# Deformable convolution block: nine 3x3 taps in 32x32 tiles, another order up to the offsets, and window sums in slabs with four product rows on GpSimd

## The reference

```python
h = gelu(conv1x1(x, proj1)); u = h
h = dwconv5x5(h, conv0)                      # pad 2
# deformable convolution, 8 groups of 8 channels, 3x3 points
xproj = h @ inproj + b                       # the "values"
x1 = gelu(layernorm(dwconv3x3(h)))
offset = x1 @ off_w + off_b                  # 2 x 9 x 8 per pixel
m = softmax(x1 @ mask_w + mask_b)            # over the 9 points
out = sum over points of m * bilinear(xproj, point + offset)
attn = conv1x1(out @ outproj)
x = conv1x1(u * attn, proj2) + shortcut
t = t + gru_like_attention(layernorm(t))     # 256 tokens per image
t = t + moe_top2_of_8(layernorm(t))          # 64 wide experts
```

## Time and profile before

| | us |
|---|---|
| median of 3 runs | 105.86 (105.59 to 106.24) |
| the profiled execution | 105.47 |
| its span, first to last instruction | 103.8 |
| mean granted TensorE clock | 0.984 of 2.4 GHz |
| PE / DVE / ACT / POOL busy | 95.0 / 70.0 / 44.5 / 27.6 |

### The profile page before, as it was taken

The page is one execution under the profiler, slowest core; times in us unless marked ns, Lnnn a source line. Parts: engine busy times, 40 slices in busy tenths (PEclk is TensorE's granted clock), DMA queues, the critical chain, the costliest instruction groups (busy, mean ns, idle before and its releaser), DMA issues.

```text
span 103.8 us, 2125 instructions
## 1 busy us (share of the span) xinstructions
PE 95.0 (91%) x843; PEld 64.3 (62%) x847; DVE 70.0 (67%) x157; ACT 44.5 (43%) x96; POOL 27.6 (27%) x37
## 2 busy tenths in 40 slices
PE   4999969999989999998999999899899999889990
PEld 1545526477646698995777776448596886664340
DVE  1359676824128999999999733477942569946871
ACT  1362054379449670000000204588842798796000
POOL 7295900000001919057897400000000000500000
PEclk9999999999859999999999999999999999999999
DMA  1999000000146526530000000000000000000002
GB/s 41 392 350 352 8 0 6 0 6 0 51 133 209 192 70 189 163 115 0 0 3 0 0 0 9 0 0 0 0 0 0 0 6 0 0 0 0 0 3 101
DMA packets 3226, 6.22 MB, mean 60 GB/s; under 512 B 528, under 2 KB 1296, under 8 KB 3216
## 3 DMA queue, kind: packets, MB, share of 16 engines
q1 hardware_dynamic: 2784, 4.67, 13.8%
q10 hardware_dynamic: 432, 1.42, 3.8%
HBM read 5.16 MB, written 0.93 MB: 59 GB/s over the span
## 4 chain that ended last, share of the span: by engine, by line
PE 61%; DVE 21%; issue 8%; ACT 6%; POOL 1%; DVEq 0%
PE ps L1121 60%; DVE prod L902 3%; DVE ym L873 2%; DVE terms L882 2%; ACT prod L712 2%; POOL prod L542 1%; ACT prod L768 1%; DVE lmax L857 1%; DVE smax L949 1%; DVE psum_p L887 1%; DVE prod L983 1%; DVE prod L987 1%; DVE prod L823 1%; PE ps L1449 1%; DVE rsum L893 1%
## 5 line engine op out<-in xcount | busy, mean ns | idle before, releaser
L1121 PE MATMUL ps<-prod,wts 128*128 128x256 f32 (+1 forms) x116 | 25.4, 394 | 1.2 <-POOL prod L542 0.6
L1121 PEld LDWEIGHTS ps<-prod,wts 128*128 128x128 f32 (+1 forms) x116 | 16.6, 174 | 8.2 <-POOL prod L542 2.6
L1121 PE MATMUL ps<-terms,wts 64*128 64x256 f32 (+4 forms) x104 | 17.4, 354 | 0.9 <-ACT prod L768 0.5
L1121 PEld LDWEIGHTS ps<-terms,wts 128*128 128x128 f32 (+1 forms) x104 | 13.8, 189 | 3.5 <-ACT prod L768 0.9
L902 DVE TENSOR_TENSOR prod<-v_win,ps 128x1280 f32<-128x1280 f32 x10 | 14.3, 1462 | 0.0
L542 POOL TENSOR_TENSOR prod<-prod 128x512 f32<-128x512 f32 x9 | 11.5, 1278 | 5.3 <-DVE prod L902 4.8
L533 POOL TENSOR_TENSOR terms<-ym,hat 128x864 f32<-128x864 f32 x2 | 5.8, 2892 | 22.4 <-DVE ym L873 22.4
L699 ACT ACTIVATE samp_t<-ps 128x256 f32<-128x256 f32 x2 | 1.3, 636 | 23.2 <-PE ps L1121 23.2
L1121 PE MATMUL ps<-idle 128*128 128x512 bf16 x25 | 8.5, 478 | 1.4 <-DVE idle L774 1.3
L614 POOL TENSOR_TENSOR terms<-terms 128x256 f32<-128x256 f32 x2 | 1.4, 724 | 30.5 <-DVE terms L999 30.5
L1121 PEld LDWEIGHTS ps<-idle 128*128 128x128 bf16 x29 | 3.2, 117 | 6.0 <-issue 3.2
(11 more groups left out here) (170 smaller groups left out, 149.0 us busy)
## 6 DMA issues: line engine op xcount, KB each, us to landing
v_win<-v_padded SPq DMA_DIRECT2D x20, 128.0 KB, 2.7
wts<-in_w ACTq DMA_DIRECT2D x1, 984.0 KB, 8.4
wts<-in_w SPq DMA_DIRECT2D x1, 640.0 KB, 7.7
v_padded<-s_v SPq DMA_DIRECT2D x1, 400.0 KB, 7.8
wts<-in_w ACTq DMA_DIRECT2D x1, 280.0 KB, 4.0
x_in<-in_x SPq DMA_DIRECT2D x1, 256.0 KB, 3.1
v_padded<-v_tok SPq DMA_DIRECT2D x4, 64.0 KB, 2.0
out<-res SPq DMA_DIRECT2D x2, 128.0 KB, 1.7
```

The costliest lines, as they stand in the source:

```text
L1121: return nc.tensor.matmul(out_, lhsT, rhs, start=start, stop=stop, skip_group_check=True)
```

## The change

Three parts. (1) All nine 3x3 taps run in tiles; `acc3` on DVE and its centring matmuls go. The bias of the convolution enters as `b_dwc`. (2) Up to the offsets the order is another: combos stand right behind `conv5` on TensorE and ACT copies them; the rows of the biases (`b_row`) are split into bf16 parts on GpSimd; variance, bias and values are interleaved, and the keep-warm matmuls there go ("weights" has 8 instead of 10). Offsets of half 0 stand ahead of the bias of half 1. SP stores the values of both halves before the first `v_win`. (3) All terms are DVE's, half 0 complete before half 1. Rows 3 and 4 of each half's products are GpSimd's, from a copy of their weights in SBUF (`a5_copied`); the other three are DVE's; nothing is merged. The sum over the 25 products of a half is 100 matmuls on 32x32 tiles into four banks ("slabs"), copies to SBUF, and four 128x32 matmuls (`sum_slabs`). The shortcut matmul moves from the middle of the weights into `close_l0`.

```diff
-PE5, PE3 = 20, 8
+PE5, PE3 = 20, 9
+ROWS = ((0, 1, 3, 2, 4), (0, 1, 3, 2, 4))
+POOLED = (3, 4)
-WARM = {"projection": 8, "conv5": 2, "v": 1, "offsets": 1, "offsets1": 1, "weights": 10, "close_l0": 2, "route": 4}
+WARM = {"projection": 8, "conv5": 2, "weights": 8, "close_l0": 2, "route": 4}
...
+            def products(bl, dy):
+                pool.wait_ge(v_windowed[bl], 16 * BH * K5)
+                pool.wait_ge(a5_copied, bl + 1)
...
+                g.tensor_tensor(prod[:, bl, dy, :, :].rearrange("p d (x c) -> p d x c", c=GC), win,
+                                weights.unsqueeze(3).broadcast_to([P, K5, XG, GC]),
+                                ALU.mult).then_inc(pool_prod_done, 1)
+            pool.wait_ge(terms_done, K3 * BL)
+            for bl in range(BL):
+                for dy in POOLED:
+                    products(bl, dy)
...
+            for bl in range(BL):
+                softmax(bl)
+                masked_hats(bl)
+                for jx in (1, 0, 2):
+                    window_terms(bl, jx)
+            flags(0)
+            flags(1)
+            for bl in range(BL):
+                for dy in range(K5 - len(POOLED)):
+                    products(bl, dy)
             mask_sums(0)
             mask_sums(1)
+            inverse_sums(0)
+            inverse_sums(1)
+            copy_slabs(1, 1)
             normalise(0)
             normalise(1)
...
+            conv5()
+            combos()
+            sum_taps5(0)
+            sum_taps5(1)
+            pe.wait_ge(diag3_set, 1)
+            pe.wait_ge(combos_copied, 1)
+            conv3(0)
+            conv3(1)
+            sum_taps3(0)
+            sum_taps3(1)
+            pe.wait_ge(w_loaded[2], 16)
+            pe.wait_ge(ones_set, 1)
+            pe.wait_ge(b_row_step, 3 * PARTS - 2)
+            variance1(0)
+            offset_bias(0)
+            variance1(1)
+            values(0)
+            values(1)
+            offsets(0)
+            offset_bias(1)
+            offsets(1)
...
+            def slab_tiles(bl, at, groups):
+                dy = ROWS[bl][at]
...
+                for dx in range(K5):
+                    n = at * K5 + dx
+                    o0, o1 = row_group(n % TG)
+                    for r in groups:
+                        p0, p1_ = row_group(r)
+                        last = mm(slab_bank(bl, r)[o0:o1, :], ident4[p0:p1_, :], prod[p0:p1_, bl, dy, dx, :],
+                                  n < TG, n >= K5 * K5 - TG)
...
+            window_sum(0)
+            window_sum(1)
+            sum_slabs(0)
+            sum_slabs(1)
             to_channels(0)
             project(0)
             to_channels(1)
             close_l0(0)
```

More of the change, by code:

```diff
@@ L119, in conv_attn_moe @@
         h_dense = sb("h_dense", [P, BL, HW])
[L120 to L124, removed]
+        b_dwc = sb("b_dwc", [P, 1])
+        ln_room = sb("ln_room", [P, 4 * BL, HW])
+        sq, lnv, rstd, xn = (ln_room[:, i * BL:(i + 1) * BL, :] for i in range(4))
         x1 = sb("x1", [P, BL, HW])
@@ L640, in _, with square @@
                 a.activation(by_tap3[:, bl, 0:TG // 2, :], tap3_banks(bl, 0, TG // 2), ACT.Copy).then_inc(out3_act, 1)
-            def square(bl, src, dst, ready, done):
+            def square(bl, src, dst, ready, done, bias=0.0):
                 act.wait_ge(ready, bl + 1)
-                a.activation(dst[:, bl, :], src, ACT.Square).then_inc(done, 1)
+                a.activation(dst[:, bl, :], src, ACT.Square, bias=bias).then_inc(done, 1)
             def inverse_std(bl, log, dst, ready, between, done, src=None):
@@ L663, in _, with over @@
             a.preload_act_table_set(LN_EXP)
+            def over(bl):
+                act.wait_ge(abs_done, bl + 1)
+                a.activation(s_pos[:, bl, :, :].rearrange("p c n -> p (c n)"), o_abs[:, bl, :], ACT.Relu,
+                             bias=w("minus_one"), accum_out=over_sum[:, bl:bl + 1]).then_inc(over_done, 1)
             def hats(bl):
@@ L683, in hats @@
                     far_hats(0, hats_done)
+                    over(0)
+                    over(1)
                 act.wait_ge(lsub_done, bl + 1)
@@ L735, in _ @@
             hats(1)
-            over(0)
-            over(1)
+            copy_a5(0)
+            copy_a5(1)
+            copy_slabs(0, 1)
+            copy_slabs(0, 0)
+            copy_slabs(1, 0)
             samples(0)
@@ L826, in _ @@
             for bl in range(BL):
-                dve.wait_ge(h_ready, bl + 1)
-                taps(bl, PE3, K3, acc3, hpad, "w3", "b_dw", acc3_done)
-            for bl in range(BL):
                 dve.wait_ge(taps3_done, bl + 1)
                 v.tensor_copy(by_tap3[:, bl, TG // 2:TG, :], tap3_banks(bl, TG // 2, TG)).then_inc(out3_dve, 1)
-            dve.wait_ge(w_loaded[1], 16)
-            dve.wait_ge(w_loaded[2], 16)
-            bias_row()
             def normed1(bl):
                 dve.wait_ge(rstd1_done, bl + 1)
[L837 to L845, removed]
+                dve.wait_ge(combos_copied, 1)
+                v.scalar_tensor_tensor(out=xn[:, bl, :], in0=d1_ps(bl), scalar=b_dwc[:, 0:1], in1=rstd[:, bl, :],
+                                       op0=ALU.add, op1=ALU.mult).then_inc(xn_done, 1)
             normed1(0)
-            copy_combos()
             normed1(1)
@@ L1221, in _, with offsets @@
                        b_row[:, C:C + OM].unsqueeze(1).broadcast_to([PARTS, 2, OM]), True, False)
-            pe.wait_ge(v_copied, 1)
-            keep_warm(WARM["offsets"], bank(0, 0))
-            for bl in range(BL):
-                if bl:
-                    keep_warm(WARM["offsets1"], bank(0, 0))
+            def offsets(bl):
                 pe.wait_ge(x1_done, bl + 1)
@@ new lines, in window_sum @@
+            def window_sum(bl):
+                pe.wait_ge(ident4_set, 1)
+                pe.wait_ge(far_set, BL)
+                first = 0
+                if bl:
+                    pe.wait_ge(a5_copied, BL)
+                    pe.wait_ge(prod_done, K5 - len(POOLED))
+                    first = 2
+                    for at in range(first):
+                        slab_tiles(bl, at, range(TG - 1))
+                    pe.wait_ge(slabs_act, 1)
+                    for at in range(first):
+                        slab_tiles(bl, at, (TG - 1,))
+                for at in range(first, K5):
+                    slab_tiles(bl, at, range(TG))
@@ L1278, in to_channels, with sum_slabs @@
+            def sum_slabs(bl):
+                pe.wait_ge(slabs_act, (2, 3)[bl])
+                if bl:
+                    pe.wait_ge(slabs_dve, 1)
+                for r in range(TG):
+                    o0, o1 = row_group(r)
+                    last = mm(bank(bl, 2)[o0:o1, 0:VW], ident4[:, :], by_slab[:, bl, r, :])
+                last.then_inc(sum_done, 1)
             def to_channels(bl):
```

222 lines of the change are left out of this document (88 added, 134 removed).

## The result

| | before | after |
|---|---|---|
| median of 4 runs each, same chip | 105.77 us (105.59 to 106.24) | 101.32 us (100.31 to 102.25) |
| ratio, with 95% interval | | 0.954 (0.946 to 0.962) |
| the profiled execution, its span | 105.47, 103.8 | 101.25, 99.6 |
| mean granted TensorE clock in it | 0.984 | 1.000 |

The forecast of 100.9 us is 0.4 from the median.

What follows compares the result with a forecast made beforehand. No engine bounds throughout; the chain alternates between TensorE and DVE. Offsets 2.25 earlier, terms 2.2, square of half 1 at 61.0 for 65.92: 5.0 gained, profiled 105.47 to 100.5, forecast 100.9, range 99.4 to 104.5.

Steps and rivals of the forecast that it cites:

- The start: Up to the offsets: tap records +0.35, centring -1.15, combos +0.3; `offsets(0)` starts at 24.9, 2.25 earlier.
- Rival (e): `offsets(0)` doesn't start earlier, combos or bias rows being late: up to 2.25 lost, 103.2; chance 0.24 shared with other cases.
- The clock: In `offsets(0)`, TensorE's clock stays at the lower level, taking 2.82; full clock would give 0.85 more.
- rival (c): TensorE's clock: falling after 50.5 gives 102.6, not falling in `offsets(0)` 100.1; chance of 102 to 104.8, shared: 0.24.
- Worth nothing either way: Terms split with GpSimd or all on DVE: 12.3 against 12.4 from the end of `offsets(0)`.
- GpSimd's products: Window stage: four products at 2.95 each, back to back from 40.1, ending at 51.9.
- (a): GpSimd's products are slow, 4.28 each: 5.3 later, 106.2, no change; chance 0.10 shared with full (b).
- (d): GpSimd's and DVE's products shut each other out: 109.7, slower than before; chance 0.08 shared with (a) beyond 4.5.
- 400 tile matmuls, 8.6: Window sums on TensorE: 400 records at 0.0215, waiting 1.3 in all, ending at 52.8.
- rival (b): TensorE bound in tiles: 0.035 a record gives 105.2 (chance 0.10 with full (a)), middle 0.028 gives 102.2 (0.24, shared).
- The tail: After the last window sum: copies, slab sums, exposed projection and shortcut put the square of half 1 at 61.0.
- Windows and bias rows: Window loads, issued by 40.1, hidden by 1.7; bias rows on GpSimd ready by 14 to 15, hidden.

Runs made afterwards that it cites:

- e10_tap8: Kernel after with the ninth 3x3 tap back on DVE and its centring matmuls on `acc3` back on TensorE: 102.19 us, ratio 0.960.
- e4_plain: Kernel after, but half 1's first two rows wait for the bank and take all four row groups together: 101.53 us, ratio 0.959.
- e1_early: Kernel before with only the first part (nine taps, new order, bias rows on GpSimd), window stage unchanged: 102.90 us, ratio 0.974.
- e2_early_terms: As `e1_early`, with all terms on DVE: 102.27 and 102.53 us at full clock, 104.93 and 105.14 at mean clock 0.967.
- e6_dense: Kernel after, but GpSimd multiplies by 1280 separate columns instead of 160 repeated weights, output not the reference's: 100.26 us, one execution.
- e7_pairs: Kernel after with two columns `dx` per tile matmul, 240 records for 400, eight slab-summing matmuls for four: median 103.35 us, 99.64 to 100.59 near full clock.
- e9_after_again: Kernel after, unchanged, measured once more: 101.38 us, ratio 0.960.
- e5_shift: Kernel after with 40 more load-and-matmul pairs on TensorE well ahead of the window stage: 100.5 us, one execution.

## Why the prediction was right, and where its steps were not

**The start.** Right in place: `offsets(0)` waits for ACT, at 25.30 for the forecast 24.9. Combos cost nothing instead of 0.3. It was late by 0.4 all the same, in two pieces. The norm's logarithm came at 21.32 for 21.2: 144 tap records took 3.44 for the 3.1 forecast, since the price of 0.0215 from 128 records did not hold (0.0239), and that used up what the combos had not cost. And ACT's run from there to the end of the table load, taken to stay at 3.03, took 3.32: `offset_bias(0)` now stands between the two variances on TensorE, and the logarithm of half 1 waits for the second (started at 22.41, released by TensorE). `e10_tap8` prices tap and centring together: the change gained 0.44 there, where +0.35 and -1.15 had promised 0.8. Rival (e) fell.

**The clock.** The forecast kept `offsets(0)` at the lower level, 2.82; it ran at the upper one in 1.74, and gave 1.07 more. In the page of `e4_plain` the clock falls in the same place, from about 25 to 32 us, `offsets(0)` takes 2.80, and the time is 101.98 against 101.02 at full clock. So the new order does not exclude the fall. It makes it rarer, as far as the runs tell: no execution of the kernel before whose clock is on record has a mean over 0.984, and eight of ten of the kernel after have 0.997 or more. The second half of rival (c), no fall in `offsets(0)`, thus came true, but not its 100.1, since the tiles took back what the clock gave. What decides between two executions of one kernel stayed open.

**The terms.** "Worth nothing either way" was 0.3 too low, by `e1_early` against `e2_early_terms`. The lock on DVE was rightly read. By the Trainium skill ("SBUF — State Buffer", section SBUF: two separate sides) GpSimd's and DVE's operations with two SBUF inputs exclude each other; `e1_early` has the waits, the kernel after has none.

**GpSimd's products.** Mis-sized: 2.43 for 2.95. The term was worked out from merges and terms, whose operands are all separate columns, and `e6_dense` gives 2.92 for such operands (it reads them from another tile as well). By the Trainium skill ("GPSIMD Engine Reference", section Performance versus the Vector engine) the estimate was 2.81; that fits neither of the two kinds, and lies nearer to the separate one. Rivals (a) and (d) fell: the four come back to back, and DVE's stay at 1.47 beside them.

**TensorE's tiles.** This is the step that failed: "400 tile matmuls, 8.6". They took 10.73, 0.0268 a record, close to rival (b)'s middle of 0.028. The records alone were as cheap as forecast or cheaper where they alternate freely (0.0204 over the first 200 of `e4_plain`); what came on top were two stops, 1.2, for which the forecast had no term (by the reading above TensorE waits for its own program there), and slower records behind the split, some 0.6. The forecast had TensorE waiting for GpSimd at the end; GpSimd was done at 48.78. By the Trainium skill ("TensorE: Matmul & The Clock Gate", section Wait — 56ns, not 53.3ns?) starts lie at least about 25 ns apart; here 200 records took 20.4 ns each, so the trace disagrees, each record counted as one matmul. The stage's end, 53.0 for 52.8, was right by errors that cancelled: GpSimd's products were forecast to end 3.1 later than they did (0.9 of it the start), and TensorE's records to take 2.1 less than they did. That the time came within 0.4 is in part luck: TensorE could start on the tiles 0.6 earlier than forecast only since the clock had given 1.07. In `e4_plain`, where it did not, the sums end at 53.61 instead of 52.94.

**The tail.** From the last sum to the square of half 1 it was 8.6 for 8.2. That, and the 0.2 by which the sums ended late, make the 0.6 by which the square came later than forecast (61.59 for 61.0). The clock in the tail stayed up.

**Windows and bias rows.** Both hidden, as said: SyncE's queue is done with the loads at 40.5 (40.1 forecast) and no product waits for a window; the bias rows are ready at 14.74 and asked for at 21.2.

## What to carry to other kernels

Read how far the engine behind the one you relieve is from being the bound: GpSimd took 5.6 us of products from DVE, and TensorE behind them left 1.7 of it. The part that puts the critical matmul directly behind the operation it waits for was worth more than all the new work-sharing (2.9 of 4.5, about 1.1 of it by the clock). When many small matmuls run back to back, count all the instructions, since at 21 ns a record TensorE can stop for its own program, and then fewer, wider records gain (`e7_pairs`, at full clock). Time an edit in several executions, since a fall of the clock 40 us behind it can cost more than it gave (`e7_pairs`: 3.4, against the 0.8 by which the square of half 1 came earlier).

## What the runs showed of the hardware

- TensorE stopped for 0.15 to 1.0 us among small tiles, in six traces of five kernels: twice, 126 or 127 records apart, in the kernel after, `e9_after_again` and `e5_shift`, and once in `e4_plain`, `e6_dense` and `e10_tap8`. Moving the count by 40 or by 12 moved the stops by as much. In the kernel after and in `e5_shift` each stop ended 1.3 to 1.5 us after a packet of 16384 bytes had landed on the instruction queue. With records of 35 ns (`e7_pairs`) there was no stop.
- A 32x32 tile record of 256 columns took 20.4 ns, of 512 columns 35.4 ns. Twenty that followed each other in one row group took 33.0 ns from start to start, against 22.9 for the same twenty in four groups.
- A GpSimd product of 128x1280 in fp32 took 2.43 us with each weight repeated eight times and 2.92 with separate weights. DVE's products with one operand in PSUM were not slowed by it (1.47 with and without).
- With a mean clock of 0.966 an execution took 0.9 us more than at full clock where the fall lay at 25 us (`e4_plain`) and 3.4 more where it lay at 93 us (`e7_pairs`, profiled); what decides between two executions is open.
